# Causal attention with its scores in two float32r parts instead of three bfloat16 parts

## The reference

```python
c_kv = x @ W_kv_down
k_rope = rotary(c_kv @ W_k_rope); q_rope = rotary(x @ W_q_rope)
k, v = c_kv @ W_k_up, c_kv @ W_v_up            # (B, T, 16, 8)
q = x @ W_q
scores = einsum('bqhd,bkhd->bhqk', q, k)
scores = (scores + einsum('bqr,bkr->bqk', q_rope, k_rope)[:, None]) / sqrt(8 + 32)
scores = where(causal, -inf, scores)
w = softmax(scores, axis=-1)
attn = einsum('bhqk,bkhd->bqhd', w, v)
x = x + attn @ W_o
```

## Time and profile before

| | us |
|---|---|
| median of the runs (2 runs, 2378.56 and 2379.85) | 2379.2 |
| profiled execution, its time | 2384.68 |
| profiled execution, span of the core | 2382.9 |
| causal attention, from the first load (113.86) to the last exponential (861.3) | 747.4 |
| matmul busy (TensorE), VectorE, ScalarE over the span | 1876.4, 1447.0, 1192.9 |

### The profile page before, as it was taken

How to read it: one execution, slowest core, us unless ns; L and a number is a source line. 1 busy time by engine, 2 the same in 40 slices (tenths; PEclk the granted TensorE clock), 3 DMA queues, 4 the chain that set the end, 5 groups by cost and what they waited for, 6 DMA issues and landing times. The chain is left out here.

```text
span 2382.9 us, 66311 instructions
## 1 busy us (share of the span) xinstructions
PE 1876.4 (79%) x26357; PEld 1132.2 (48%) x26357; DVE 1447.0 (61%) x2903; ACT 1192.9 (50%) x2328; POOL 455.3 (19%) x532
## 2 busy tenths in 40 slices
PE   4557999999999973488854699999999997438875
PEld 2225887787787753356533122222222222326554
DVE  4564665565555325833216899999999993584320
ACT  2403665555555641022224388888888886103222
POOL 2400000000000000167753000000000000016775
PEclk9857999999999985588777699999999998557877
DMA  3341232222321001133333000000000000113333
GB/s 88 112 105 45 64 82 61 65 74 64 74 65 59 17 1 38 42 69 64 57 56 114 33 15 29 15 29 15 25 19 19 25 3 1 38 28 80 65 56 60
DMA packets 87902, 117.44 MB, mean 49 GB/s; under 512 B 13832, under 2 KB 56720, under 8 KB 85264
## 3 DMA queue, kind: packets, MB, share of 16 engines
q1 hardware_dynamic: 64176, 96.07, 13.9%
q0 software_dynamic: 23424, 17.12, 5.5%
HBM read 80.88 MB, written 33.33 MB: 48 GB/s over the span
## 5 line engine op out<-in xcount | busy, mean ns | idle before, releaser
L1088 DVE TENSOR_REDUCE mx<-wide 128x2 f32<-128x1024 f32 x512 | 603.7, 1221 | 45.1 <-PE wide L1016 33.0
L1116 ACT ACTIVATE pT<-bank 128x512 f32<-128x512 f32 x1024 | 555.2, 594 | 85.2 <-PE bank L1009 77.6
L834 ACT ACTIVATE pT<-bank 128x512 f32<-128x512 f32 (+3 forms) x768 | 375.3, 491 | 361.5 <-PE bank L671 301.8
L691 PE MATMUL bank<-pT,vst 128*32 128x256 f32 (+3 forms) x3072 | 476.6, 330 | 16.1 <-issue 16.0
L637 PE MATMUL wide<-k_max,q_max 120*32 120x512 bf16 (+3 forms) x3072 | 448.3, 350 | 12.1 <-DVE mx L768 10.1
L666 PE MATMUL bank<-q_rope,k_rope 128*32 128x512 bf16 (+3 forms) x3072 | 417.6, 330 | 1.4 <-issue 1.0
L671 PE MATMUL bank<-q_exp,k_exp 128*32 128x512 bf16 (+3 forms) x3072 | 414.1, 329 | 2.3 <-issue 1.9
L1016 PE MATMUL wide<-k_st,q_st 48*128 48x512 bf16 x1024 | 351.8, 399 | 37.0 <-DMA k_st<-qk_parts 24.0
L1009 PE MATMUL bank<-q_st,k_st 51*128 51x512 bf16 x1024 | 355.1, 387 | 21.1 <-ACT pT L1116 5.2
L765 DVE TENSOR_REDUCE mx<-wide 128x1 f32<-128x640 f32 (+3 forms) x256 | 261.2, 1024 | 141.0 <-PE wide L637 140.3
L1025 PE MATMUL bank<-pT,vst 128*32 128x256 f32 x4096 | 328.1, 392 | 0.1
(11 more groups left out here) (228 smaller groups left out, 2407.2 us busy)
## 6 DMA issues: line engine op xcount, KB each, us to landing
qk_parts<-parts SPq DMA_DIRECT2D x16, 768.0 KB, 3.5
q_max<-rope_parts SPq DMA_DIRECT2D x24, 256.0 KB
k_max<-rope_parts SPq DMA_DIRECT2D x24, 256.0 KB
q_exp<-rope_parts SPq DMA_DIRECT2D x16, 256.0 KB
k_exp<-rope_parts SPq DMA_DIRECT2D x16, 256.0 KB
xn_rows<-xn SPq DMA_DIRECT2D x8, 512.0 KB, 3.2
w1b<-in_L_ffn_w SPq DMA_DIRECT2D x16, 256.0 KB
w2b<-in_L_ffn_w SPq DMA_DIRECT2D x16, 256.0 KB
```

Of the source, the lines that this page charges most:

```text
L691: ins = e.matmul(bank[2 + J][32 * j:32 * (j + 1), qs], vst[par][:, kc, j, :], pT[:, u % NPB, qs], start=(kc == 0 and half == 0), stop=(las ...
L834: e.activation(pT[:, u % NPB, q0:HALF], bank[u % 2][:, q0:HALF], ACT.Exp, scale=scale).then_inc(s_p, 1)
L1088: e.tensor_reduce(mx[G % 2][:, kh, pair:GH:2, c], wide[w % 2][:, :].rearrange("p (r k) -> p r k", r=2), AX.X, ALU.max).then_inc(s_sf, 1)
L1116: e.activation(pT[:, u % NPB, :], bank[u % 2][:, :], ACT.Exp, scale=scale).then_inc(s_p, 1)
```

## The change

The first attention gets a function of its own, `attend_causal`. Named by part:

- `project(True)` splits q, k and the rotary rows into two float32r parts: ScalarE's rounded copy and VectorE's residue. The second copy of ScalarE and all of GpSimd's work there are gone. The parts are stored as 4-byte numbers (`qk_split`, `rope_split`).
- One stack `q_st` and one `k_st` of 120 rows (three pairs of parts, rotary rows and head rows) serve both sides. Two more rows hold the negated maxima. Each tile of scores is one matmul over the full array of 128 columns of weights, with one more for the mask on the diagonal.
- The stacks have three buffers. The rotary rows are loaded anew where `s % 4 < 3`.
- All steps are unrolled in rounds: round t has the tiles 2t and 2t+1 of the second side, the pair of scores t+25 of the first side, and `weigh` of round t-2. A step has 24 rounds.
- GpSimd splits the maxima in two, TensorE turns them, ScalarE copies them, and GpSimd sends the rows, for each half of a step.
- `y_all`, the result, is written over `v_all`.

The diff, cut to its core (the lines of `attend` that it removes are those printed above):

```diff
-MAX_PAIRS = [(0, 0), (0, 1), (1, 0)]
+RPAIRS = [(0, 0), (0, 1), (1, 0)]
...
         v_all = sb("v_all", [P, B, NG, NC, GH * HD])
-        y_all = sb("y_all", [P, B, NG, NC, GH * HD])
+        y_all = v_all
...
-        rope_dram = nc.dram_tensor("rope_parts", [3, B, 2 * DR, T], BF16, kind="Internal").ap()
+        split_dram = nc.dram_tensor("qk_split", [2, 2, B, P, T], F32, kind="Internal").ap()
+        rope_dram = nc.dram_tensor("rope_split", [2, B, 2 * DR, T], F32, kind="Internal").ap()
...
-            parts = [buf(f"parts{i}", [P, 2, 3, T], BF16) for i in two]
-            rparts = [buf(f"rparts{i}", [2 * DR, 3, T], BF16) for i in two]
+            parts = [buf(f"parts{i}", [P, 2, 2, T], F32R) if latent else buf(f"parts{i}", [P, 2, 3, T], BF16) for i in two]
+            rparts = [buf(f"rparts{i}", [2 * DR, 2, T], F32R) for i in two] if latent else None
...
+                            if latent:
+                                cols = slice(h * HALF, (h + 1) * HALF)
+                                e.tensor_tensor(parts[par][:, t, 1, cols], bank[2 + n % 2][:, :],
+                                                parts[par][:, t, 0, cols].bitcast(F32), ALU.subtract).then_inc(s_r1, 1)
...
-                        for n in range(NQ):
+                        for n in range(NQ if not latent else 0):
...
+                                e.wait_ge(s_r1, PRIME + b * NQ + (t + 1) * NHALF)
+                                e.dma_start(split_dram[t, :, bass.ds(b, 1), :, :].rearrange("n o p t -> p (o n) t"),
+                                            parts[par][:, t, :, :].bitcast(F32)).then_inc(s_out[par], 16)
...
+        def attend_causal():
+            scale = float((HD + DR) ** -0.5)
+            LEAD, NBUF = 25, 3
+            FIRST, SECOND = 8, 16
+            NP = FIRST + SECOND
+            LAST = STEPS * NP
+            KS = NROWR + len(RPAIRS) * HD
+            KROW = KS + 2
...
+            q_st = [buf(f"q_st{i}", [P, NHALF, GH, HALF], F32R) for i in range(NBUF)]
+            k_st = [buf(f"k_st{i}", [P, GH, T], F32R) for i in range(NBUF)]
...
+            def unit(u):
+
+                H = half_of(u // 2)
+                kc, j = divmod(u - 2 * begins(H), GH)
+                return H // 2, H % 2, kc, j, max(0, (kc - H % 2 * CPH) * P)
+
+            def score_at(w):
+
+                G = half_of(w)
+                n = w - begins(G)
+                if G % 2 == 0:
+                    j, c = divmod(n, 2)
+                    return G, j, [(2 * c, 0, (2 * c + 1) * P, True), (2 * c + 1, 0, (2 * c + 2) * P, True)]
+                j, c = divmod(n, CPH)
+                return G, j, [(c, 0, HALF, False), (c, 1, (c + 1) * P, True)]
+
+            turn_at = {max(begins(G + 1) - LEAD + 2, begins(G - 1) + 3 if G >= 2 else -LEAD): G for G in range(2 * STEPS)}
+            ends = {begins(H + 1): H for H in range(2 * STEPS)}
...
+                    def t_score(u):
+                        s, J, kc, j, q0 = unit(u)
+                        at, diag = s % NBUF, kc >= J * CPH
                         if diag:
+                            e.matmul(bank[u % 2][:, q0:q0 + P], identb[:, :], mask_kq[:, :], start=True, stop=False,
+                                     skip_group_check=True)
+                        e.matmul(bank[u % 2][:, q0:HALF], k_st[at][0:KROW, j, kc * P:(kc + 1) * P],
+                                 q_st[at][0:KROW, J, j, q0:HALF], start=not diag, stop=True,
+                                 skip_group_check=True).then_inc(s_st, 1)
+
+                    def score(w, side):
+                        G, j, sides = score_at(w)
+                        c, kh, width, diag = sides[side]
+                        at, col = G // 2 % NBUF, side * HALF
                         if diag:
+                            e.matmul(wide[w % 2][:, col + width - P:col + width], identb[:, :], mask_qk[:, :],
+                                     start=True, stop=False, skip_group_check=True)
+                        return e.matmul(wide[w % 2][:, col:col + width], q_st[at][0:KS, G % 2, j, c * P:(c + 1) * P],
+                                        k_st[at][0:KS, j, kh * HALF:kh * HALF + width], start=not diag, stop=True,
+                                        skip_group_check=True)
+
+                    def weigh(quad, half):
+                        for i in range(GH):
+                            u = quad * GH + i
+                            s, J, kc, j, q0 = unit(u)
+                            mid = (q0 + HALF) // 2
+                            qs = slice(mid, HALF) if half else slice(q0, mid)
+                            ins = e.matmul(bank[2 + J][32 * j:32 * (j + 1), qs], vst[s % 2][:, kc, j, :], pT[:, u % NPB, qs],
+                                           start=(kc == 0 and half == 0), stop=(kc == (J + 1) * CPH - 1 and half == 1),
+                                           tile_position=(0, 32 * j), skip_group_check=True)
+                            if half:
+                                ins.then_inc(s_pv, 1)
+
+                    for t in range(-LEAD, LAST + 10):
+                        w, u = t + LEAD, 2 * t
+                        tiles, scores = 0 <= t < LAST, w < LAST
+                        if tiles:
+                            H = half_of(t)
+                            if t == begins(H):
+                                e.wait_ge(s_row[H % 2], (H // 2 + 1) * 16)
+                            if u >= 2:
+                                e.wait_ge(s_p, PRIME + u - 1)
+                            t_score(u)
+                        if scores:
+                            if w % NP == 0:
+                                e.wait_ge(s_q[w // NP % NBUF], PRIME + loaded(w // NP, n_q))
+                                e.wait_ge(s_k[w // NP % NBUF], PRIME + loaded(w // NP, n_k))
+                            if w >= 2:
+                                e.wait_ge(s_sf, PRIME + w - 1)
+                            score(w, 0)
+                        if tiles:
+                            if u >= 2:
+                                e.wait_ge(s_p, PRIME + u)
+                            t_score(u + 1)
+                        if scores:
+                            score(w, 1).then_inc(s_s, 1)
+                        if 0 <= t - 2 < LAST:
+                            quad, half = divmod(t - 2, 2)
+                            if t == 2:
+                                e.wait_ge(s_vz, PRIME + 4)
+                            if (t - 2) % NP == 0:
+                                e.wait_ge(s_vs, PRIME + (t - 2) // NP + 1)
+                            if half == 0:
+                                if t - 2 == begins(half_of(t - 2)) and half_of(t - 2) >= 2:
+                                    e.wait_ge(s_y, PRIME + half_of(t - 2) - 1)
+                                e.wait_ge(s_p, PRIME + (quad + 1) * GH)
+                            weigh(quad, half)
...
+                            e.wait_ge(s_m, PRIME + G + 1)
+                            dst = q_st[G // 2 % NBUF][KS:KROW, G % 2, :, :].bitcast(F32)
+                            e.dma_start(dst.rearrange("i j x -> i (j x)"), nmp[G % 2][:, :].bitcast(F32)).then_inc(s_row[G % 2], 16)
...
+                    def load_q(s):
+                        b, g = divmod(s, NG)
+                        for J in range(NHALF):
+                            cols = slice(J * HALF, (J + 1) * HALF)
+                            for n, (part, _) in enumerate(RPAIRS):
+                                rows = split_dram[0, part, b].rearrange("(g d j) t -> g d j t", g=NG, j=GH)
+                                at = NROWR + n * HD
+                                e.dma_start(q_st[s % NBUF][at:at + HD, J, :, :].bitcast(F32),
+                                            rows[g, :, :, cols]).then_inc(s_q[s % NBUF], 16)
+                                if is_new(s):
+                                    at = n * DR
+                                    src = rope_dram[part, b, 0:DR, cols].rearrange("r (o x) -> r o x", o=1)
+                                    e.dma_start(q_st[s % NBUF][at:at + DR, J, :, :].bitcast(F32),
+                                                src.broadcast_to([DR, GH, HALF])).then_inc(s_q[s % NBUF], 16)
...
+                    e.wait_ge(s_row[1], 16)
+                    load_q(2)
+                    e.wait_ge(s_one, PRIME + 3)
+                    load_k(2)
+                    for s in range(STEPS - NBUF):
+                        e.wait_ge(s_st, PRIME + 2 * NP * (s + 1))
+                        load_q(s + NBUF)
+                        load_k(s + NBUF)
```

More of the change, by code:

```diff
@@ L7 @@
 BF16 = mybir.dt.bfloat16
+F32R = mybir.dt.float32r
 I32, U32 = mybir.dt.int32, mybir.dt.uint32
@@ L398, in body @@
                                              ACT.Copy).then_inc(s_hi, 1)
-                            for h in range(NHALF):
+                            for h in range(NHALF if not latent else 0):
                                 n = t * NHALF + h
@@ L574, in attend @@
```

(35 more changed lines are left out.)

469 lines of the change are left out of this document (127 added, 342 removed).

## The result

The changed kernel takes 2413.1 us (median of 2 runs, 2410.7 to 2415.5) against 2379.2: ratio 1.0142, 95% interval 1.0098 to 1.0187. Timed once more in another set, beside new runs of the kernel before, it was 1.0109 (1.009 to 1.0128). It lies outside the range, on the side of "slower", but within 2%.

The account below looks back on a forecast made before the run. TensorE bounds causal attention. 359 rounds at 37.9 us per 24 (567), after a first exponential at 163 and with 28 at the end, put the last exponential at 758 instead of 861: −103, 2276 us; range 2170 to 2350.

Parts of the forecast that it names:

- start: first exponential: Causal attention's start: loads at 106, first score at 134 after 28 us, then 25 pairs in 29 us, first exponential at 163.
- The last 25 rounds: End of causal attention, rounds without a first side: 27 us a step, 28 us for the 25.
- rival 2: Rows of the maxima come late beside a new stack: nine steps lose 6.4 us each, +58, 2334 us; chance 0.16.
- the rows go through another queue: The argument against late rows of the maxima: they don't use the queue that carries the stack loads.
- hidden in 36: Load of a new 3.93 MB stack: 20 to 21 us, covered by the 36 us until its scores begin.
- a sign that I had named as refuting this part: A wait of `score` on a stack would refute the claim that stack loads are hidden.
- TensorE's term: TensorE's time per causal-attention step: 26.5 us streaming, 5.6 switches, 4.2 uncovered loads, 1.6 gaps; 37.9 us in all.
- rivals 3 and 5: Float32r takes two cycles a column (2509 us, chance 0.09), or runs as float32 in four passes (about 3000 us, 0.05).
- The switch from `weigh` to full arrays: TensorE, each round: 0.57 us, 0.14 more than streaming; with the switch back, 5.6 us a step.
- The bounds of 30 and 44: Limits in us per step: 30 with loads hidden and switches at half cost, 44 with switches, loads and gaps half dearer.
- Rival 4: Weight loads of full arrays stand in line with TensorE's products: +133 to +195, 2409 to 2471 us; chance 0.05.
- Rival 1: TensorE does better, 31 to 34 us a step, because switches weren't measured under pressure; 2194 us, chance 0.13.

Follow-up runs that it names:

- e2: The changed kernel without reloading the rotary rows of batches 1 to 3, so later stacks are 0.79 MB; ratio 0.9808 to the kernel before.
- e4: The changed kernel with ScalarE, not GpSimd, issuing the rows of the maxima right behind its copy; ratio 1.0493 to the kernel before.
- e13: e10 with the query stack's first half sent at once, its second half and the keys behind the row; 2266.1 us, ratio 0.9632 to the kernel before.
- e1: The changed kernel with the whole next stack held back until the row of the second half has landed; ratio 1.0193 to the kernel before.
- e14: e13 with the second step's stack sent only after the first scores; ratio 0.9651 to the kernel before.
- e3: The changed kernel with TensorE reading the scores' float32r operands as bfloat16, lower digits left out; ratio 0.9787 to the kernel before.
- e10: e9 without the causal mask ahead of the maxima; ratio 0.9769 to the kernel before.
- e9: The changed kernel with only the key stack held back until the row of the second half has landed; ratio 0.9882 to the kernel before.

## Why the prediction was wrong

The last exponential was forecast at 758 and came at 895.3, 137 us late. The parts, from the changed kernel's trace:

| step of the prediction | forecast | measured | us |
|---|---|---|---|
| start: first exponential | 163 | 175.8 | +13 |
| free step of 24 rounds, 359 rounds | 37.9 | 40.2 | +34 |
| waits for the rows of the maxima, nine steps | 0 | 49.6 idle, 28 at the low clock | +78 |
| third stack late, first interval | 0 | 2.7 idle, then the low clock; 3 by the start | +12 |

The last 25 rounds took 28, as forecast (by its own terms the sum there is 27.7 a step, or 29). Start and free step alone would have given 2276 + 13 + 34 = 2323 us, inside the range, and e2, without the holes, came to 0.9808 of the kernel before, 2333 us. The waits took it out.

**The step that failed is the wait for the rows of the maxima, which the sum put at nothing: the choice between forecast and rival 2.** It measured 78 us. The rival had the place (four rounds, 6.3 us for the row, 5.7 measured), the steps (9 with a new stack; nine holes of 2 to 6.5 us, and one of 0.2), the time that a row behind full engines takes (12.7 us; 12.1) and the hole (6.4; 6.4 in the one shown, 5.5 on average). I gave it 0.16 on one argument, "the rows go through another queue", which no row supported. The changed kernel itself refutes it for GpSimd's queue and e4 for ScalarE's, and e2, where only the rotary loads are gone, shows what the row waits for. Before, SP issued the rows ahead of the next loads in its own queue (218.50), and the wait was 13.6 us in all, one wait at the start; that this order is what protected it was not tried alone, though e13 restores it in part and has 0.7 us of row waits left.

The rival was also too cheap, 58 us for 78: it had no term for the low clock, which cost about 3 us more behind each hole.

**A second step failed, the load of a stack.** I had 20 to 21 us, "hidden in 36". A stack of 3.93 MB took 35 us for step 2 in the changed kernel (183.60 to 218.35), 34 in e1 and 35 at the start of e14. The third stack, which is sent behind a row, was late by 2.7 us, which was a sign that I had named as refuting this part; the later ones, sent at once, were not late. With the low clock behind it this is most of the 12 us of the first interval. About 3 of them are the start's: the row at 180.66 waited 4.5 us for its copy where later ones waited 7.4, so the interval begins early.

**TensorE's term was right in its mechanism, with one size off.** One cycle a column held; rivals 3 and 5 are out. The switch from `weigh` to full arrays is 0.57 us, as priced. A float32r weight load counts 0.14 us, where I took 0.105 from float32: behind 64 masks, 0.087 us each with its gap, that is 5.6 us. The 32 products without a mask ahead have gaps of 0.024, 0.8 us. Together 6.4 stand against 4.2 + 1.6 = 5.8 in the sum (most of the 16 tiles of 128 columns that I had added have a bfloat16 mask's load behind them, which doesn't show). Another 1.1 us a step had no term: the transposes of the maxima and of the result (lines 624 and 631). These are 1.7 of the 2.3 us between 37.9 and 40.2; the rest I can't place. e3 bounds all of the type's extra cost at 5.0.

The changed step alone thus lost 1.5 us to the clean step before. 18,432 columns fewer, 7.7 us, bought nothing, because loads and gaps (6.4) and switches (5.6) take 12 us beside its columns; in the step before, all that isn't columns was 4.6, and 1.4 of it transposes (lines 701 and 706), not small tiles. The bounds of 30 and 44 held the step.

Rival 4 (loads in line with products, which is also the rule of the Trainium skill, "TensorE: Matmul & The Clock Gate", section "The mechanism" under Part 3) fails here too: an unmasked product of 512 columns, 0.21 us of streaming, takes 0.24, though its load has 0.20 (PEld of lines 558 and 569). Rival 1 is out: TensorE was pressed and switched at the old price.

**Start.** The first load came at 107.9 (forecast 106) and the first scores 36 us later, where 28 were priced with bounds of 21 and 42. By e14 that is the first stack's own time and not the two stacks' sharing. The first exponential then needed 32 us instead of 29.

**Right at no cost**: ScalarE and VectorE waited for TensorE (324.7 and 228.8 us), and behind the stage nothing got longer (+31 in the whole for +34 in the stage), so neither the result over v nor GpSimd's split of the maxima shows a cost; neither was tried alone.

**Open**: why a stack has a tail of some 14 us at half of the engines' share and less (286 to 301 in e1); why rows from ScalarE's queue wait longer than GpSimd's; what the row waits for in the stack, its bytes, its number of DMAs or its broadcasts; and what made the holes of the loop before (42.5 us on average against 38.7).

## What to carry to other kernels

When a change makes loads larger or earlier, look for the small DMA on the critical path that will be in flight with them: another issuing queue is no lane of its own, but issuing the bulk behind the small one is. Hold back only as much as the deadline of the bulk allows, for its last part may come long after the time that bytes over bandwidth gives. Price a hole of TensorE with the slower clock behind it. And count columns only after loads: fewer columns in full arrays can be no faster than more in strips, where short products stand ahead of loads.

## What the hardware showed that I had not expected

- The 32 DMAs of 16 KB from GpSimd's queue landed after 2.3 us at best, 4.8 in the median and 12.4 at worst, the late ones beside a stack of 3.93 MB; from ScalarE's queue one held TensorE up to 16 us, 22 after its issue.
- That stack took 34 us in e1, with 155 to 208 GB/s until 286 us, then 116, 53, 25, 26 and 15 in windows of 3 us, and 35 us in e14 with no other stack in flight.
- Float32r streams a column per cycle in full arrays, as bfloat16 does, but its load of 128 columns counts about 0.14 us, and 32 short masks ahead of such loads cost 0.12 us each (e10, with e9 beside it).
- After 6.4 us without work TensorE ran at 1.2 GHz for about 5 us (granted clock 0.50 from 283 to 289, 0.88 in the next three). After 2.7 us without work it did so for some 13 us (218 to 232): the longer hole was not followed by the longer slow stretch.
